# Four adapted layers on one core: one block for projections and heads, adapter packs by 8 loads, output weights split in reading order

## The reference, cut to what matters

```python
x = x + einsum('bsi,boi->bso', x, weight[ids0])                       # layer 0: 512x512 weight per sample
# layer 1: attention, 32 query heads, 8 key/value heads of 128, causal
q, k, v = lora(x, wq, aq, bq), lora(x, wk, ak, bk), lora(x, wv, av, bv)
q, k = rope(q, positions), rope(k, positions)
p = softmax(where(causal & mask, q @ k.T / sqrt(128), lowest))
x = x + lora(p @ v, wo, ao, bo)                                       # rank 16, adapter picked per sample
x = x + (x @ B[ids0].T) @ A[ids0].T                                   # layer 2: rank 16
x = x + x @ W.T + b + 2 * (x @ As[ids3]) @ Bs[ids3]                   # layer 3: rank 16
# lora(x, w, a, b) = x @ w + (x @ a[ids1]) @ b[ids1]
```

## Time and profile before

| | |
|---|---|
| median of three runs | 848.53 us (847.76 to 848.71) |
| the profiled execution, its own time | 849.5 us |
| its span, first to last instruction | 847.8 us |
| projections, until PE's first score | 0 to 236.9 us |
| heads | 236.9 to about 784.9 us |
| layers 2 and 3 | about 784.9 to 847.8 us |
| PE busy over the span | 755.8 us (89%) |
| DVE, ACT, POOL busy | 63%, 38%, 35% |

### The profile page before, as it was taken

How to read it: one execution, slowest core, us unless ns; L and a number is a source line. 1 busy time by engine, 2 the same in 40 slices (tenths; PEclk the granted TensorE clock), 3 DMA queues, 4 the chain that set the end, 5 groups by cost and what they waited for, 6 DMA issues and landing times. The chain is left out here.

```text
span 847.8 us, 13367 instructions
## 1 busy us (share of the span) xinstructions
PE 755.8 (89%) x4100; PEld 623.1 (73%) x4100; DVE 536.1 (63%) x1370; ACT 324.8 (38%) x902; POOL 294.1 (35%) x265
## 2 busy tenths in 40 slices
PE   3292989879779999999999999999999999998798
PEld 2282877657567887887887888788788788876586
DVE  3251558756866667657566667666765756654883
ACT  4261525112053435335344435343534533433550
POOL 1020325253545236235326335423623532420220
PEclk8587899989889999999999999999999999999899
DMA  6573678546604122303303302312130310620502
GB/s 218 215 267 94 193 239 269 157 157 191 215 9 137 39 63 66 109 16 108 111 0 108 127 0 62 136 38 62 65 108 21 103 37 0 151 26 2 128 14 87
DMA packets 63083, 87.88 MB, mean 104 GB/s; under 512 B 20086, under 2 KB 37654, under 8 KB 59334
## 3 DMA queue, kind: packets, MB, share of 16 engines
q1 hardware_dynamic: 44338, 73.54, 28.0%
q10 hardware_dynamic: 17044, 8.46, 3.3%
q0 software_dynamic: 1664, 5.44, 2.1%
HBM read 72.45 MB, written 19.68 MB: 109 GB/s over the span
## 5 line engine op out<-in xcount | busy, mean ns | idle before, releaser
L966 POOL TENSOR_TENSOR prob<-prob,rinv 128x512 f32<-128x512 f32 x64 | 66.6, 1040 | 255.3 <-DVE rinv L1054 255.3
L907 ACT ACTIVATE ot_hi<-ps_o 128x512 fp32r<-128x512 f32 x64 | 38.1, 595 | 222.1 <-PE ps_o L1110 222.1
L1122 PE MATMUL ps_out<-wo_hi,ot_hi 128*128 128x512 f32 x256 | 102.8, 402 | 10.4 <-DVE wo_lo L1004 5.7
L959 POOL TENSOR_TENSOR qt<-qc,qs 128x512 f32<-128x512 f32 x60 | 77.9, 1298 | 70.0 <-DVE qs L993 70.0
L917 ACT ACTIVATE prob<-sm,nmax 128x128 f32<-128x128 f32 x256 | 99.8, 392 | 6.2 <-DVE nmax L1035 4.5
L1123 PE MATMUL ps_out<-wo_lo,ot_hi 128*128 128x512 f32 x256 | 101.3, 396 | 0.0
L1124 PE MATMUL ps_out<-wo_hi,ot_lo 128*128 128x512 f32 x256 | 100.8, 394 | 0.0
L78 PE MATMUL ps_q<-x1t_hi,wgt_hi 128*128 128x512 f32 x240 | 100.4, 418 | 0.0
L80 PE MATMUL ps_q<-x1t_hi,wgt_lo 128*128 128x512 f32 x240 | 95.4, 398 | 0.0
L79 PE MATMUL ps_q<-x1t_lo,wgt_hi 128*128 128x512 f32 x240 | 95.2, 397 | 0.0
L1032 DVE MEMSET gate<- 128x1 f32 x64 | 3.8, 59 | 136.9 <-PE ps_s L1091 136.9
(11 more groups left out here) (193 smaller groups left out, 1720.2 us busy)
## 6 DMA issues: line engine op xcount, KB each, us to landing
raw_w<-in_wq SPq DMA_DIRECT2D x8, 1024.0 KB, 5.3
wo_raw<-in_wo SPq DMA_DIRECT2D x8, 1024.0 KB, 4.9
raw_b<-bq_sel SPq DMA_DIRECT2D x56, 128.0 KB, 5.2
qt<-in_w SPq DMA_DIRECT2D x5, 1024.0 KB, 6.8
v_hi_d<-v_hi ACTq DMA_DIRECT2D x16, 256.0 KB, 4.6
v_lo_d<-v_lo ACTq DMA_DIRECT2D x16, 256.0 KB, 5.1
kt<-k_rot SPq DMA_DIRECT2D x16, 256.0 KB, 2.6
v_hi<-v_hi_d SPq DMA_DIRECT2D x16, 256.0 KB, 3.2
```

The costliest lines, as they stand in the source:

```text
L959: pool.tensor_tensor(qt[:, half, h, :], qc[:, :], qs[:, :], ALU.add).then_inc(q_done, 1)
L966: pool.tensor_tensor(prob[i][:, :, :], prob[i][:, :, :], rinv[i][:, :].unsqueeze(2).broadcast_to([P, G, T]), ALU.mult).then_inc(prob_done, 1)
L1122: pe.matmul(ps_out[:, :], ot_hi[:, q], wo_hi[:, h, :], start=(h == 0), stop=False)
```

## The change

1. **Packs by 8 loads.** One load per sample brings its 16 rows four times: the source is a view with a first dimension of 4 that repeats (`broadcast_to([4, R, GW])`), the destination is 64 rows of `raw_b`. The rows of a pack are in a new order, so `axn` is laid out anew, and the low rows are no longer the lower half: DVE works on all 128 rows with a column `lows` of 0 and -1 (`scalar_tensor_tensor` in place of `tensor_tensor` on 64 rows). `lows` is a new small constant, loaded from the ACT queue.
2. **One semaphore per pair** of samples, `raw_b_in[p]`, for which ACT waits piece by piece.
3. **The order on SP.** `load_x(1)` and `load_a(1)` come ahead of the pack; the pack of `j = 0` is spread: pair 0 after `load_a(1)`, pair 1 after `load_a(2)`, pairs 2 and 3 after `load_a(3)`. `a_raw` has four buffers instead of three.
4. **`bq_sel`** is laid out by group, so that a sample's rows of a group are contiguous; POOL's copy writes 8 x 16 rows of 2 KB. `load_bq` issues four loads per half, as before, now of the new kind.
5. **One block for projections and heads.** The eight PSUM banks have one set of names for both parts, and the buffers of the two parts lie over each other in SBUF as before. In place of the end of the block stand waits: PE's first `scores` waits for POOL's last rotation, PE's first two `queries` for DVE, ACT's first `wq_hi_part` for the last Q unit.
6. **The output weights.** ACT writes `wo_hi` 0, 1, 2, 3 and then `ot_hi`. DVE does part 0 alone, POOL parts 1, 2, 3. DVE's `bq_lo_part` comes after `rotate`.

```diff
-    bq_sel = nc.dram_tensor("bq_sel", (B, R, KVH * GW), F32, kind="Internal").ap()
+    bq_sel = nc.dram_tensor("bq_sel", (KVH, B, R, GW), F32, kind="Internal").ap()
...
-        raw_b_in = sem(attn, "raw_b_in")
+        raw_b_in = [sem(attn, f"raw_b_in{p}") for p in range(PAIRS)]
...
+        ps_y = [ps(attn, f"ps_y_s{i}", [P, HID]) for i in range(2)]
+        ps_x1 = ps(attn, "ps_x1_t", [P, HID])
+        ps_ax = ps(attn, "ps_ax_ao", [P, HID])
+        ps_p = [ps(attn, f"ps_p_{name}", [P, HID]) for name in ("out", "o", "q0", "q1")]
+        ps_s = [bank[:, :].rearrange("p (h t) -> p h t", t=T) for bank in ps_y]
+        ps_t, ps_ao, ps_out, ps_o, ps_q = ps_x1, ps_ax, ps_p[0], ps_p[1], ps_p[2:4]
...
-        def load_block_b(dma, j):
+        def load_block_b(dma, j, pairs):
...
-            for b in range(B):
+            for b in range(2 * pairs[0], 2 * pairs[-1] + 2):
                 pick = dma.value_load(id_rows[0:1, 1, b:b + 1], min_val=0, max_val=src.shape[0] - 1)
-                for quad in range(4):
-                    at = 32 * quad + R * (b % 2)
-                    dma.dma_start(raw_b[at:at + R, b // 2, :], src[bass.DynSlice(pick, 1), :, cols].rearrange("a r n -> (a r) n")).then_inc(raw_b_in, 16)
+                four_times(dma, b, src[bass.DynSlice(pick, 1), :, cols], raw_b_in[b // 2])
+
+        def four_times(dma, b, rows, done):
+            dma.dma_start(raw_b[4 * R * (b % 2):4 * R * (b % 2 + 1), b // 2, :], rows.broadcast_to([4, R, GW])).then_inc(done, 16)
...
         def load_bq(dma, g, h):
-            for quad in range(4):
-                dma.dma_start(raw_b[32 * quad:32 * quad + 32, 2 * h:2 * h + 2, :],
-                              bq_sel.rearrange("(c two) r n -> (two r) c n", two=2)[:, 2 * h:2 * h + 2, bass.DynSlice(g * GW, GW)]
-                              ).then_inc(bq_in[h], 16)
+            for b in range(HALF * h, HALF * (h + 1)):
+                four_times(dma, b, bq_sel[bass.DynSlice(g, 1), b], bq_in[h])
...
                 load_block_w(sp, 0)
-                    load_block_b(sp, 0)
                 load_x(1)
                 load_a(1)
+                load_block_b(sp, 0, range(0, 1))
                 load_w0(2)
                 load_x(2)
                 load_a(2)
+                load_block_b(sp, 0, range(1, 2))
                 for b in range(RAW, B):
                     load_w0(b)
                     load_x(b)
                     load_a(b)
+                    if b == 3:
+                        load_block_b(sp, 0, range(2, 4))
...
-                                act.wait_ge(raw_b_in, RAW_B_IN[j])
+                            act.wait_ge(raw_b_in[k], 32 * (j + 1))
...
-                                dve.tensor_tensor(pack[low, k, :], raw_b[low, k, :], pack[low, k, :].bitcast(F32), ALU.subtract).then_inc(b_lo_done, 1)
+                            dve.scalar_tensor_tensor(pack[:, k, :], pack[:, k, :].bitcast(F32), lows[:, 0:1], raw_b[:, k, :],
+                                                     ALU.mult, ALU.add).then_inc(b_lo_done, 1)
...
-                    pool.dma_start(bq_sel[b:b + 1], bq[pick]).then_inc(gathered, 16)
+                    pool.dma_start(bq_sel[:, b], bq[pick].rearrange("a r (g n) -> (a g) r n", n=GW)).then_inc(gathered, 16)
...
                 @block.tensor
                 def _(pe):
+                    project_tensor(pe)
...
+                        else:
+                            pe.wait_ge(k_mult, 3 * (VU + G - 1 + n))
...
+                        if isinstance(t, int) and t == 0:
+                            pe.wait_ge(k_done, VU + G)
...
-                                wo_hi_part(g, 0)
-                                wo_hi_part(g, 2)
+                                for h in range(G):
+                                    wo_hi_part(g, h)
                             if not first or b >= 1:
                                 ot(t - 1, None if not first else t - 1)
                             if b == 1:
-                                wo_hi_part(g, 1)
-                                wo_hi_part(g, 3)
                                 ao_hi_part(g)
...
-                                for h in range(G // 2, G):
-                                    pool.wait_ge(wo_hi_done, G * g + 2 * (h - G // 2) + 2)
+                                for h in range(1, G):
+                                    pool.wait_ge(wo_hi_done, G * g + h + 1)
...
-                            if b == 2:
-                                wo_lo_part(g, 1)
-                            if not last and b % 2:
-                                bq_lo_part(PAIRS * g + b // 2 + 1, b // 2)
...
                             if not (last and b >= HALF):
                                 rotate(t, (b // HALF + 1) % 2, i)
+                            if not last and b % 2:
+                                bq_lo_part(PAIRS * g + b // 2 + 1, b // 2)
                             if b == 1:
                                 wo_lo_part(g, 0)
```

More of the change, by code:

```diff
@@ L95, in program @@
         twin = sb(whole, "twin", [P, 3])
+        lows = sb(whole, "lows", [P, 1])
         l2b_sel = sb(whole, "l2b_sel", [P, KC, B, R])
@@ L124, in program @@
         a_lo = [sb(early, f"a_lo{i}", [P, KC, 3, R], F32R) for i in range(2)]
-        axn = [sb(early, f"axn{i}", [P, 3, 4, 2, R], F32R) for i in range(2)]
+        axn = [sb(early, f"axn{i}", [P, 3, 2, 4, R], F32R) for i in range(2)]
         early.close()
@@ L240, in program @@
[L240 to L249, removed]
@@ L274, in program @@
[L274 to L277, removed]
+            ps_a = ps_ax[:, 0:3 * R].rearrange("p (n r) -> p n r", r=R)
+            ps_at = ps_ax[:, T:4 * T].rearrange("p (n t) -> p n t", t=T)
+            lora_ids_in = sem(attn, "lora_ids_in")
+            ids_in = sem(attn, "ids_in")
+            w0_first_in = [sem(attn, f"w0_first_in{k}") for k in range(KC)]
+            consts_in = sem(attn, "consts_in")
@@ new lines, in program @@
+            x_in = [sem(attn, f"x_in{b}") for b in range(B)]
+            xt_in = [sem(attn, f"xt_in{i}") for i in range(RAW)]
+            w0_in = [sem(attn, f"w0_in{i}") for i in range(RAW)]
+            a_in = [sem(attn, f"a_in{b}") for b in range(B)]
+            ident_ready = sem(attn, "ident_ready")
+            xt_hi_done = sem(attn, "xt_hi_done")
+            xt_lo_done = sem(attn, "xt_lo_done")
+            wt_hi_done = sem(attn, "wt_hi_done")
+            wt_lo_done = sem(attn, "wt_lo_done")
@@ new lines, in program @@
+            y_ready = sem(attn, "y_ready")
+            x1_done = sem(attn, "x1_done")
+            x1t_ready = sem(attn, "x1t_ready")
+            x1t_hi_done = sem(attn, "x1t_hi_done")
+            x1t_lo_done = sem(attn, "x1t_lo_done")
+            zeroed = sem(attn, "zeroed")
+            a_hi_done = sem(attn, "a_hi_done")
+            a_lo_done = sem(attn, "a_lo_done")
+            ax_ready = sem(attn, "ax_ready")
+            axn_hi_done = sem(attn, "axn_hi_done")
+            axn_lo_done = sem(attn, "axn_lo_done")
@@ new lines, in program @@
+            axt_ready = sem(attn, "axt_ready")
+            axt_done = sem(attn, "axt_done")
+            w_hi_done = sem(attn, "w_hi_done")
+            w_lo_done = sem(attn, "w_lo_done")
+            b_hi_done = sem(attn, "b_hi_done")
+            b_lo_done = sem(attn, "b_lo_done")
+            p_ready = sem(attn, "p_ready")
+            v_hi_done = sem(attn, "v_hi_done")
+            v_lo_done = sem(attn, "v_lo_done")
+            scaled = sem(attn, "scaled")
+            v_out = [sem(attn, f"v_out{i}") for i in range(VR)]
@@ L279, in parts @@
+            k_mult = sem(attn, "k_mult")
+            k_done = sem(attn, "k_done")
+            k_out = [sem(attn, f"k_out{i}") for i in range(2)]
+            tables_in = sem(attn, "tables_in")
+            tab = sem(attn, "tab")
+            sines = sem(attn, "sines")
             def parts(b):
@@ L920, in slots @@
                             if b < HALF and not last:
+                                if first and b == 0:
+                                    act.wait_ge(p_ready, KU + G)
                                 act.wait_ge(q_ready, B * g + b + 1)
@@ L1523, in constants @@
     gather = np.stack([(row % R_PACK == col % R_PACK) & (col // R_PACK % 2 == i) for i in range(2)], 1).astype(np.float32)
-    return {"ident_c": np.eye(P, dtype=np.float32), "causal_c": causal, "rope_c": rope, "gather_c": gather, "twin_c": twin}
+    lows = np.where(np.arange(P)[:, None] % (4 * R_PACK) >= 2 * R_PACK, -1.0, 0.0).astype(np.float32)
+    return {"ident_c": np.eye(P, dtype=np.float32), "causal_c": causal, "rope_c": rope, "gather_c": gather, "twin_c": twin, "lows_c": lows}
 def kernel(**inputs):
```

932 lines of the change are left out of this document (443 added, 489 removed).

## The result

The changed kernel takes 824.62 us (median of four runs, 822.15 to 828.61) where the kernel before took 848.62 beside it: a ratio of 0.9716, 95% interval 0.9671 to 0.9762. A second series of six runs gave 826.15 us and 0.9724 (0.9700 to 0.9748). The forecast was 807.0 us with a range of 791 to 823: the direction is right, but 24 us were saved instead of 41.8, and the time lies 1.6 us above the range. The profiled execution took 825.5 us, span 823.8. Every run reported here was a fast one except one of the four of e1, which took 1476.49 us: e1's median of 804.04 us counts it (803.46 without it), its ratio does not.

A forecast was written before the change was run, and what follows sets the result against it. PE was taken as full in the heads but waiting in the projections, largely on slow issuing of loads. Terms summed to 41.8 us: 849.5 - 41.8 = 807.7, on the median 806.7 us, range 791 to 823.

The forecast's parts named there:

- first wait: In the projections, PE's second turn of x1 comes at 27.9 instead of 41.41 us: 13.5 us saved, bounds 11 and 16.
- second wait: At step 4 to 5 of PE's turns of x1, most of the delay for pack 1 goes: 14.2 us saved.
- V units: From 110 to 155 us, bound by stores of V and POOL's copies: 0 saved, between -4 and +3.
- K and Q: In the 19 units of K and Q, earlier packs and stores shorten PE's waits: 6.3 us saved, lower bound 0.
- one block: Between projections and heads, PE's first score waits for POOL at 233.58 instead of 236.91: 3.3 us saved, from 2 to 5.
- behind the first score: In the heads, PE's wait for the part of `wo_lo` that DVE wrote last goes: 4.5 us saved, 3 to 6.
- the price of issuing: On SP, a sample's read and one load cost 1.16 instead of 2.42 us, a block 9.3 instead of 19.3 us.
- How the load moves: The new pack load uses four of 16 DMA engines: 101 GB/s, 1.3 us a load, 10.4 us a block.
- the wide case: Rival for the pack loads: dealt to all engines, 53.3 us saved, 795.2 us; chance 22%.
- the transfers bind: Rival for the projections: four engines have no room, V's buffers and `w0` come late, 27 us saved, 821.5 us; chance 20%.
- The slower rival: Rival for the pack loads: fewer engines still, deciding from 54 GB/s; on one engine 905 us; chance 3%.
- the forecast's own case: Whole kernel with pack loads on four engines: 41.8 us saved, 800 to 815 us; chance 45%.

The follow-up runs named there:

- e1: The changed kernel with each sample's load turned round, rows outside and copies inside (16 x 4 x 512): 804.04 us, ratio 0.9446.
- e12: The changed kernel itself, unedited, run again in another series: ratio 0.9724 to the kernel before.
- e5: The changed kernel with the projections in a block of their own again, so the engines meet ahead of the heads: 829.69 us, ratio 0.9749.
- e3: The changed kernel with wide loads (rows outside, copies inside) and the eight adapter numbers read into SP registers once: 799.19 us, ratio 0.9404.
- e9: The changed kernel with two loads a sample of 2 x 16 x 512, slowest dimension 2: 869.33 us, ratio 1.0242.
- e4: The changed kernel with each sample's load as four loads of 16 rows again, in the new order: 835.43 us, ratio 0.9836.

## Why the prediction was wrong where it was

The sum in its own terms, from the spans (847.8 - 823.8 = 24.0 us):

| term | forecast | after | e12, the same kernel | e1 |
|---|---|---|---|---|
| first wait | 13.5 | 11.0 | 12.0 | 13.9 |
| second wait (turn 1 to 7) | 14.2 | 8.9 | 8.5 | 19.2 |
| V units | 0 | -2.4 | -1.8 | -3.3 |
| K and Q | 6.3 | -1.3 | 0.2 | 9.0 |
| one block | 3.3 | 3.3 | 3.3 | 3.3 |
| behind the first score | 4.5 | 4.5 | 2.0 | 3.9 |
| sum | 41.8 | 24.0 | 24.2 | 46.0 |

Of the 17.8 us that are missing, K and Q have 7.6, the second wait 5.3, the first wait 2.5 and the V units 2.4. Two executions of the same kernel differ by up to 2.5 us in one term, so the two small ones say little by themselves. The step that failed first is the price of issuing, the largest miss is K and Q.

- **How the load moves: right.** Four engines, 98 GB/s, 2.67 us a pair (forecast 101 and 2.6). The Trainium skill, "DMA: Bandwidth & Descriptors", section "Why a DMA increments its semaphore by 16 and not by 1", has the number of engines from the slowest dimension; pair spacings of 5.35 and 2.67 us for 2 and 4 agree, and with 16 only the issuing is left to see (1.0 to 1.5 us). It also says that on the queues of SP and ACT these are the lowest-numbered engines; the 95 GB/s with several loads outstanding agree with one fixed set of four, but no run here shows which.
- **Issuing: the first step that failed.** I took the pitch of a sample as 2.42 - 3 x 0.42 = 1.16 us, with the new load at the old one's price. The load costs 0.62 instead of 0.37, and the read behind it 0.73 instead of 0.27: 1.87 us, 13.8 us a block instead of 9.3. The first store of K is issued 14.9 us after unit 1 (152.09 - 137.17), where the forecast had 10.3 (165 - 154.72).
- **K and Q, 6.3 us: the largest miss.** The mechanism was the right one (wait of 7 us at unit 17 forecast, 8.10 measured; half clock after it), but laid onto a timetable without delays ahead of it. The late first store lands in 5.5 us, POOL waits 9.91 us for it and DVE 7.27 for POOL, PE waits 3.8 us at 162 and 168 us, and pack 4 is issued 44.0 us after unit 1 instead of 37.8. The miss of 7.6 us is all there at unit 17, which starts 65.2 us after unit 1 instead of 57.7. In e1, whose loads are wide and cost SP less, pack 4 is issued 36.7 us after unit 1, and K and Q give 9.0 us, where the wide case had 13.
- **Second wait, 14.2 us: give-back too small.** 5 us were given back; the step cost 7.3 us over the normal pace, so 11.9 us were saved there. The forecast had the first pair of pack 1 about in time; ACT waited 5.18 us for it and 2.05 us for the second. Another 3.0 us were lost from turn 1 to 3 against the kernel before, which the sum left out: pack 0's other pairs stand ahead of `w0(3)` and `w0(4)` on the four engines (ACT waits 1.74 us for `xt(4)` and 1.59 for `w0(4)`). With wide loads the step from turn 2 to 3 is back at 7.84 us.
- **First wait: right, at its lower bound** (11.0, and 12.0 in e12). 11 was the bound for data late by 2.5 us; ACT splits `w0(2)` at 26.31 instead of 23.8. e1's turn at 27.47 is the forecast's 27.9.
- **V units: within -4 to +3.** They lose 2.4 us in after and 3.3 in e1. ACT waits for the stores of V there in every kernel, 16.3 us in all before, 15.1 in after, 18.9 in e1; that they take up what comes early is likely, but not shown.
- **One block: right** (e5). **Heads: the sum within reach, its parts not.** 4.5 us in this profile, 2.0 in e12. The moved `bq_lo_part` was put at nothing, for its reader is 3 us away; but it runs beside POOL's rotation, which then mostly takes 1.85 us, and PE waits 2.3 us for rotations in all (2.9 in e12).
- **The rivals.** The time came near where "the transfers bind" put it (821.5), and for its stated reason in part. Its terms were added up wrongly: 13.5 + 8 - 4 + 3.3 + 3.3 + 4.5 are 28.6 us and not 27, so 819.9. The wide case (795.2) comes nearest to e1, at 804, and e3, at 799. The slower rival put its turning point at 54 GB/s; e9 at 49 GB/s is 2.4% slower than before.

The range failed since the forecast's own case was costed on the favourable side in three steps, and the rival that did so less had 20%.

## What to carry to other kernels

A load that repeats rows should have the rows outside and the copies inside: the same bytes and instructions, 20.6 us between the two here. Fewer, larger loads pay less, and can cost time, when they spread over few engines: against loads of 16 rows (e4) eight narrow loads gained 11 us on four engines and eight wide ones 31, while two loads a sample on two engines lost 34. Look at both limits, SP's time for a sample and the transfer's, and at what stands behind them on the queue. An operation that is moved may be cheap itself and still slow another engine's that it now runs beside. When a mechanism delays one place, carry the delay through the later places before pricing them.

## What the hardware showed that was not expected

- A register read on SP takes 0.27 us behind a load with a slowest dimension of 16 or more, and 0.73 to 0.77 us behind one of 2, 4 or 8 (single reads are longer, up to 1.10 us in after and 1.33 us in e1). Within after, the four reads from 25 to 31 us (the first behind a wide load):

```profile
L182 SPq TENSOR_LOAD <-id_rows x4: 278/745/771, 25.0 to 30.2; - x4
```

The same section of the Trainium skill says that the issuing sequencer writes the part of the increment that the unused engines don't; that may be what the read waits for, but no run here shows it.

- Issuing isn't one price: 0.37 us for 16 rows, 0.54 for 16 x 4, 0.62 for 4 x 16, 0.72 for 8 x 4, all out of `bk`. Out of `bq_sel`, where a sample's rows of a group are contiguous, 4 x 16 takes 0.53 us and 16 x 4 takes 0.59 in pack 4 (0.55 and 0.54 in the heads): there the wide load is no cheaper for SP.
